# The second attention's order on TensorE: scores and value products unit by unit instead of two by two

## The chip, the cores and the metric

One Trainium2 chip, of which the kernel uses one core. The metric is the time of the core for one execution, in microseconds (us). The engines are TensorE (PE; its weight loads are listed apart, as PEld), VectorE (DVE), ScalarE (ACT), GpSimd (POOL), and SyncE (SP), which issues DMA transfers. TensorE's granted clock in the profile is 1.00 for 2.4 GHz and 0.50 for 1.2 GHz.

## The reference

Two transformer layers on x (4 batches of 256 rows of 256), each with an attention to a context of 1601 rows per batch and a mixture of experts. All is float32; a residual is added after each of the four parts.

```
x = x + L0_xattn(layernorm(x), ctx, mask)       # one head over 256 columns
x = x + L0_ffn(layernorm(x), ...)               # 16 experts, dense
x = x + L1_xattn(layernorm(x), ctx, mask, ...)  # 16 heads of 16 columns
x = x + L1_ffn(layernorm(x), ...)               # 16 experts, top 2
```

The change touches the third part alone:

```
q, k, v = proj(hs, Wq, bq), proj(at, Wk, bk), proj(at, Wv, bv)   # (B, 16, L, 16)
scores = clip(einsum('bhsd,bhtd->bhst', q, k) / 4, -50, 50)
scores = clip(where(attend, scores, -10000), -50, 50)
probs  = softmax(scores)
ctx    = einsum('bhst,bhtd->bhsd', probs, v)
delta  = layernorm(residual_scale * (ctx @ Wo.T + bo))
```

## The kernel before

The kernel is one program with one instruction list per engine; the lists are written out by hand and tied together by semaphores. Its stages are the first attention, the first experts (up to about 424 us), the second attention (424 to 647 us), and the routed experts.

The second attention works in *units*. There are 16 jobs (4 batches by 4 groups of 4 heads, `NJ`), and each job walks over the context in 13 tiles of up to 128 rows (`MT`; the last has 65), so there are 208 units (`NALL`), counted through as x or y. Per unit:

- `qk(x)` (L964): TensorE computes the scores of 4 heads as 4 matmuls (L986) of 49 rows, in the two row halves of the array: keys x 256 queries each, into a PSUM slot of two banks. There are 3 slots (`RING`), so it first waits until the exponential of unit x - 3 is done (L979).
- ScalarE (loop at L1458) takes the exponential of the 128 x 1024 scores into one of 6 buffers `p32` (L1465, `PBUF`), after the value products of unit x - 6 have left it.
- VectorE, `clip(x)` (L1980), clips it in place (L1984). The clip of the exponential stands for the clip of the scores; a column of ones in the values gives the softmax's sum.
- `pv(x)` (L1013): after the clip, TensorE multiplies it with the values: 4 matmuls in the source, 8 in the trace (L1028), each 17 columns wide, in the four column strips of the array, and accumulated over the 13 units of a job in bank 6 or 7.

TensorE runs the value products 4 units behind the scores (`PV_LAG`). Between them it does the other work of the stage, placed by unit number: `flip` (L1032) transposes a finished job's result, 7 units into the next job; `early(y)` (L940) makes queries; `between(y)` (L1080) does, for each finished batch, the transposes, the output projection (L1050), the transposes of the normalized rows (L1057), the router's logits and the ranks. ScalarE and VectorE have lists of the same names with their shares of that work, placed by unit number too, and POOL takes the reciprocal square roots of the normalization (L370 to L378). SP loads the keys of a job after the scores of three jobs before, counted on `sc_rdy`, and the values of a batch counted on `pv_done`.

Of the kernel before, what the change touches and what calls it, by code (L numbers as in the profile page):

```python
# [30 lines left out]
MT = -(-M // P)  # L31
# [24 lines left out]
NALL = NJ * MT  # L56
# [5 lines left out]
PV_LAG = 4  # L62
EVAC_AT = 3
FLIP_AT = 7
# [14 lines left out]
def build(nc, a, out, stop="D"):  # L79
# [9 lines left out]
    with ExitStack() as ctx:  # L89
# [211 lines left out]
        def at(x):  # L301

            return x // MT, x % MT

        def rows_of(m):

            return TAIL if m == MT - 1 else P
# [41 lines left out]
        def keys_in(job):  # L349

            return sum(96 + 16 * new_bar(j) for j in range(job % KSL, job + 1, KSL))
# [337 lines left out]
        def _(pe):  # L689
# [223 lines left out]
            def pair_T(q, bank):  # L913
                pe.wait_ge(ln_xn, 2 * NT + 2 * q + 2)
                for k in range(KT):
                    for j in range(2):
                        mm = pe.transpose(ps[:, bank, (2 * k + j) * P:(2 * k + j + 1) * P], xn[:, 2 * q + j, k * P:(k + 1) * P], ident[:])
                mm.then_inc(ln_T, 1)

            def first_queries(b, c, o):  # L920
                s, w = slice(b * SEQ, (b + 1) * SEQ), slice(c * P, (c + 1) * P)
                for k in range(KT):
                    mm = mm3(pe, o, wgh[:, k, w], wgl[:, k, w], xTh[:, k, s], xTl[:, k, s], k == 0, k == 1)
                mm.then_inc(Q_rdy, 1)

            def queries(n, bank):
                half, t = n // KT, n % KT
                s, w = slice(half * 512, half * 512 + 512), slice(t * P, (t + 1) * P)
                for k in range(KT):
                    mm = mm3(pe, ps[:, bank, :], wqh[:, k, w], wql[:, k, w], xTh[:, k, s], xTl[:, k, s], k == 0, k == 1)  # L930
                mm.then_inc(Q_rdy, 1)
# [8 lines left out]
            def early(y):  # L940
                if y == 0:
                    pe.wait_ge(ln_lo, 6)
                    queries(0, 7)
                elif y == 3:
                    queries(1, 6)
                elif y == 9:
                    pe.wait_ge(q_lo, 6)
                    for c in range(2):
                        first_queries(1, c, ps[:, 7, c * SEQ:(c + 1) * SEQ])
                elif y == 23:  # L950
                    pe.wait_ge(cx_rdy, 1)
                    pair_T(2, 6)
                elif y == 36:
                    pe.wait_ge(cx_rdy, 2)
                    pair_T(3, 7)
                elif y == 49:
                    pe.wait_ge(cx_rdy, 3)
                    pe.wait_ge(ln_lo, 8)
                    queries(2, 6)
                elif y == 61:  # L960
                    pe.wait_ge(cx_rdy, 4)
                    queries(3, 7)

            def qk(x):  # L964

                job, m = at(x)
                b, g = job // NG, job % NG
                if m == 0:
                    pe.wait_ge(k_in[job % KSL], keys_in(job))
                    if b == 0 and g == 0:  # L970
                        pe.wait_ge(q_lo, 4)
                    elif b == 0:
                        pe.wait_ge(q_in[g], 16 * (3 * HG + (1 if g % 2 else 0)))
                    elif b == 1 and g == 0:
                        pe.wait_ge(q_lo, 10)
                    elif b == 2 and g == 0:
                        pe.wait_ge(q_in[NG], 16 * (3 * HG * NG + 1))
                if x >= RING:
                    pe.wait_ge(p_exp, x - RING + 1)  # L979
                elif x == 1:  # L980
                    pe.wait_ge(add_rdy, 4)
                rows = rows_of(m)
                for c in range(2):
                    for t in range(2):
                        r = slice(64 * t, 64 * t + KR)
                        mm = pe.matmul(ps[0:rows, 2 * (x % RING) + t, c * SEQ:(c + 1) * SEQ], kst[r, job % KSL, c, m * P:m * P + rows],  # L986
                                       qst[r, b, 2 * g + c, :], start=True, stop=True, skip_group_check=True)
                mm.then_inc(sc_rdy, 1)

            def free_again(job):  # L990

                b, r = job // NG - 1, job % NG
                if job == 0:
                    pe.wait_ge(q_lo, 6)
                elif job == 1:
                    pe.wait_ge(q_lo, 10)
                elif job in (2, 3):
                    pe.wait_ge(ln_lo, 5 + job)
                elif job == 4:
                    pe.wait_ge(q_lo, 11)  # L1000
                if 0 < b and r == 1 and b < NB:
                    pe.wait_ge(lg_ev, min(b, NB - 2))
                if 0 <= b < NB - 1:
                    if r == 1:
                        pe.wait_ge(cT_ev, 2 * b + 2)
                    elif r == 2:
                        pe.wait_ge(dl_ev, 2 * b + 2)
                if 0 < b < NB - 1 and r == 3:
                    pe.wait_ge(pre_ev, b)
                if 0 < b and r == 0:  # L1010
                    pe.wait_ge(ln_lo, 8 + 2 * b)

            def pv(x):  # L1013

                job, m = at(x)
                b, g = job // NG, job % NG
                if m == 0:
                    if g == 0:
                        pe.wait_ge(v_in[b % 2], 16 * (b // 2 + 1))
                    if job >= 2:  # L1020
                        pe.wait_ge(cx_rdy, job - 1)
                    free_again(job)
                pe.wait_ge(p_clip, x + 1)
                rows = rows_of(m)
                for j in range(HG):
                    at_ = (m * NH + g * HG + j) * VW
                    c, t = j // 2, j % 2
                    mm = pe.matmul(ps[32 * j:32 * j + VW, 6 + job % 2, 0:SEQ], vsl[0:rows, b % 2, at_:at_ + VW],  # L1028
                                   p32[0:rows, x % PBUF, (2 * t + c) * SEQ:(2 * t + c + 1) * SEQ], start=m == 0, stop=m == MT - 1, skip_group_check=True)
                mm.then_inc(pv_done, 1)  # L1030

            def flip(job):  # L1032

                pe.wait_ge(oS_rdy, job + 1)
                for st in range(2):
                    mm = pe.transpose(ps[:, 6 + job % 2, SEQ + st * P:SEQ + (st + 1) * P], oS[:, st * P:(st + 1) * P], ident[:])
                mm.then_inc(oT_rdy, 1)
# [42 lines left out]
            def between(y):  # L1080

                b, o = y // UB - 1, y % UB
                t = 2 * b
                spare = ps[:, 6 + (y // MT - 1) % 2, :]
                if 0 < b < NB - 1 and o == 36:
                    pe.wait_ge(cx_rdy, y // MT)
                    ranks(b, t - 2, t, spare)
                if 0 < b < NB - 1 and o == 10:
                    pe.wait_ge(cx_rdy, y // MT)
                    logits(b - 1, spare)  # L1090
                if 0 <= b < NB - 1:
                    if o == 13 - 1:
                        if b:
                            pe.wait_ge(lg_ev, b)
                        else:
                            pe.wait_ge(q_lo, 12)
                        ctx_T(t, 2, spare)
                    elif o == 23:
                        pe.wait_ge(cx_rdy, y // MT)
                        ctx_out(t, 0, 2, spare[:, 0:D])  # L1100
                    elif o == 24:
                        ctx_out(t + 1, 1, 2, spare[:, D:2 * D])
                    elif o == 51:
                        pe.wait_ge(cx_rdy, y // MT)
                        rows_T(t, 2, spare)

            for x in range(0, NALL + PV_LAG, 2):
                for y in (x, x + 1):
                    if y < NALL:
                        qk(y)  # L1110
                for y in (x, x + 1):
                    early(y)
                    between(y)
                    if y >= MT + FLIP_AT and (y - FLIP_AT) % MT == 0:
                        flip((y - FLIP_AT) // MT - 1)
                    if y >= PV_LAG:
                        pv(y - PV_LAG)
            flip(NJ - 1)

            def gates(h, k, bank):  # L1120
# [1262 lines left out]
```

## Time and profile before

| | us |
|---|---|
| median of 3 runs | 746.43 |
| lowest, highest | 744.87, 751.39 |
| the profiled execution | 751.78 |
| its span in the trace | 750.0 |
| second attention, first scores to last value products | 424.3 to 647.4 |

The profile is of one execution. Times in it are microseconds from the start of its span unless ns is given. An instruction is named by its line and by the tiles that it writes and reads. An idle time in square brackets is that of the engine just before the instruction, with what ended it; "issue" means nothing that the profile shows. Where a timeline merges instructions that follow each other closely, it gives the first start, the time from there to the last end, and their count.

### The profile page before, as it was taken

To read this page: it belongs to the slowest core of one execution; us is meant where nothing else is said; L and a number is where in the kernel's file an instruction comes from. 1 tells how busy PE (TensorE), PEld (TensorE's weight loads), DVE (VectorE), ACT (ScalarE), POOL (GpSimd) and SP (SyncE) were. 2 spreads that over 40 slices of the span, in tenths; PEclk is the share of its full clock that TensorE was granted. 3 is DMA by queue.
4 is the path that set the end of the run, shared out by engine and by line. 5 is a ranking of instruction groups with operands and counts; after the bars stand their busy time and mean duration, and the time that the engine had idled before them with its cause. 6 is when DMAs were issued, how large, how long until landed. Compare 5 with 4: busy or idle time off the path is not lost.

```text
span 750.0 us, 14926 instructions
## 1 busy us (share of the span) xinstructions
PE 685.2 (91%) x5499; PEld 533.6 (71%) x5499; DVE 535.0 (71%) x1176; ACT 379.8 (51%) x564; POOL 176.5 (24%) x220
## 2 busy tenths in 40 slices
PE   4799989898889999999999699999999999989990
PEld 3799989898678888888888455455455454567870
DVE  5776747568486666666666888769788888875655
ACT  2633423244322222223232699879899999533550
POOL 5472615440000000000000050002302703542651
PEclk9999999999999999999999999979999999999995
DMA  7358474832717777677778949986888850374545
GB/s 249 123 180 264 140 263 147 272 124 90 221 47 244 225 263 244 218 214 240 256 238 147 168 82 149 207 130 99 183 157 176 126 96 2 119 296 135 158 133 189
DMA packets 55275, 131.55 MB, mean 175 GB/s; under 512 B 10007, under 2 KB 36103, under 8 KB 51631
## 3 DMA queue, kind: packets, MB, share of 16 engines
q1 hardware_dynamic: 51950, 123.32, 61.9%
q0 software_dynamic: 2256, 6.18, 2.3%
q10 hardware_dynamic: 1008, 1.25, 0.5%
q8 instruction: 38, 0.62, 0.4%
q14 instruction: 23, 0.18, 0.1%
HBM read 79.09 MB, written 48.82 MB: 171 GB/s over the span
## 4 chain that ended last, share of the span: by engine, by line
PE 73%; DVE 12%; POOL 5%; issue 4%; ACT 4%; DMA 2%; SPq 0%; POOLq 0%; DVEq 0%; ACTq 0%
PE ps L684 16%; PE ps L686 15%; PE ps L685 15%; PE ps L1028 9%; PE ps L986 6%; PE ps L1216 3%; DVE p L1984 2%; PE ps L1232 2%; PE ps L768 1%; ACT p L1465 1%; POOL nv L370 1%; POOL na L373 1%; PE ps L1200 1%; PE ps L1050 1%; POOL na L374 1%
## 5 line engine op out<-in xcount | busy, mean ns | idle before, releaser
L1465 ACT ACTIVATE p<-ps 128x1024 f32<-128x1024 f32 (+1 forms) x208 | 193.3, 1052 | 12.8 <-PE ps L986 12.8
L1984 DVE TENSOR_SCALAR p<-p 128x1024 f32<-128x1024 f32 (+1 forms) x208 | 139.0, 688 | 20.1 <-ACT p L1465 19.2
L1028 PE MATMUL ps<-p,vsl 128*17 128x256 f32 (+1 forms) x1664 | 118.0, 390 | 7.5 <-DVE p L1984 6.0
L1371 ACT ACTIVATE hh<-h 128x512 fp32r<-128x512 f32 x50 | 31.6, 632 | 132.3 <-DVE h L1851 115.3
L370 POOL TENSOR_SCALAR nv<-mv 128x2 f32<-128x2 f32 x8 | 9.5, 1187 | 354.7 <-DVE mv L1914 208.0
L986 PEld LDWEIGHTS ps<-qst,kst 49*128 49x128 f32 (+1 forms) x832 | 57.5, 184 | 49.0 <-issue 26.6
L986 PE MATMUL ps<-qst,kst 49*128 49x256 f32 (+1 forms) x832 | 81.9, 312 | 1.3 <-DVE qst L1927 0.8
L684 PE MATMUL ps<-xTh,w_hi 128*128 128x512 f32 x200 | 79.8, 399 | 1.5 <-DVE h L1847 0.9
L685 PE MATMUL ps<-xTl,w_hi 128*128 128x512 f32 x200 | 79.0, 395 | 0.0
L686 PE MATMUL ps<-xTh,w_lo 128*128 128x512 f32 x200 | 78.9, 395 | 0.0
L1028 PEld LDWEIGHTS ps<-p,vsl 128*17 128x17 f32 (+1 forms) x1664 | 35.6, 96 | 48.0 <-DVE p L1984 13.7
L1853 DVE TENSOR_TENSOR hl<-h,hh 128x512 fp32r<-128x512 f32 x50 | 34.6, 692 | 36.6 <-ACT hh L1371 36.6
L684 PE MATMUL ps<-w_hi,hh 128*128 128x256 f32 x200 | 56.6, 283 | 1.5 <-DVE hl L1853 1.5
L1847 DVE TENSOR_TENSOR h<-silu,ps 128x512 f32<-128x512 f32 x50 | 34.4, 688 | 31.9 <-PE ps L686 20.8
L685 PE MATMUL ps<-w_lo,hh 128*128 128x256 f32 x200 | 56.3, 281 | 0.0
L686 PE MATMUL ps<-w_hi,hl 128*128 128x256 f32 x200 | 56.2, 281 | 0.0
L627 POOL TENSOR_TENSOR cNl<-raw,cNh 128x1024 fp32r<-128x1024 f32 (+1 forms) x16 | 31.4, 1985 | 68.0 <-ACT cNh L1295 68.0
L684 PEld LDWEIGHTS ps<-xTh,w_hi 128*128 128x128 f32 x200 | 37.8, 189 | 9.5 <-DVE h L1847 1.7
L686 PEld LDWEIGHTS ps<-xTh,w_lo 128*128 128x128 f32 x200 | 37.6, 188 | 8.9
L685 PEld LDWEIGHTS ps<-xTl,w_hi 128*128 128x128 f32 x200 | 37.7, 189 | 6.6
L684 PEld LDWEIGHTS ps<-w_hi,hh 128*128 128x128 f32 x200 | 37.7, 188 | 4.8 <-DVE hl L1853 2.7
L1367 ACT ACTIVATE silu<-ps 128x512 f32<-128x512 f32 x50 | 30.0, 599 | 18.4 <-PE ps L686 17.8
(310 smaller groups left out, 1539.3 us busy)
## 6 DMA issues: line engine op xcount, KB each, us to landing
x_slots<-blank SPq DMA_DIRECT2D x20, 1032.0 KB, 5.9
kst<-k_hi SPq DMA_DIRECT2D x64, 200.2 KB
w_raw<-in_w SPq DMA_DIRECT2D x25, 384.0 KB, 3.6
v_one<-vst SPq DMA_DIRECT2D x4, 1768.0 KB, 10.0
vsl<-v_one SPq DMA_DIRECT2D x4, 1768.0 KB, 16.5
kst<-k_lo SPq DMA_DIRECT2D x32, 200.2 KB
raw<-in_ctxN SPq DMA_DIRECT2D x12, 512.0 KB, 5.7
e_w<-in_w SPq DMA_DIRECT2D x2, 3072.0 KB, 16.1
```

Of the source, the lines that this page charges most:

```text
L627: pool.tensor_tensor(cNl[:, c0:c0 + w, :], src, cNh[:, c0:c0 + w, :].bitcast(F32), ALU.subtract).then_inc(ctx_split, 1)
L684: e.matmul(o, lh, rh, start=first, stop=False, skip_group_check=True)
L685: e.matmul(o, lh, rl, start=False, stop=False, skip_group_check=True)
L686: return e.matmul(o, ll, rh, start=False, stop=last, skip_group_check=True)
L986: mm = pe.matmul(ps[0:rows, 2 * (x % RING) + t, c * SEQ:(c + 1) * SEQ], kst[r, job % KSL, c, m * P:m * P + rows], qst[r, b, 2 * g + c, :], ...
L1028: mm = pe.matmul(ps[32 * j:32 * j + VW, 6 + job % 2, 0:SEQ], vsl[0:rows, b % 2, at_:at_ + VW], p32[0:rows, x % PBUF, (2 * t + c) * SEQ:(2 ...
L1367: act.activation(silu[:, half, :], ps[:, 4, :], ACT.Silu).then_inc(silu_rdy, 1)
L1371: act.activation(hh[:, half, :], h32[:, half, :], ACT.Copy).then_inc(hh_rdy, 1)
L1465: act.activation(p32[0:rows, x % PBUF, :], psf[0:rows, bank * 512:bank * 512 + 1024], ACT.Exp, scale=0.25).then_inc(p_exp, 1)
L1847: dve.tensor_tensor(h32[:, half, :], silu[:, half, :], ps[:, 5, :], ALU.mult).then_inc(mul1_rdy, 1)
L1853: dve.tensor_tensor(hl[:, half, :], h32[:, half, :], hh[:, half, :].bitcast(F32), ALU.subtract).then_inc(hl_rdy, 1)
L1984: dve.tensor_scalar(t, t, CLO, CHI, ALU.max, ALU.min).then_inc(p_clip, 1)
```

## The change

TensorE's main loop over the units went in steps of two: scores of x and x + 1, then, for x and then for x + 1, the work placed at that unit (`early`, `between`, `flip`) and the value products of four units before. It now goes in steps of one: scores of y, the work placed at y, value products of y - 4. The instructions, their waits and the lists of all other engines are the same. So two units that ran as scores, scores, values, values run as scores, values, scores, values; work placed at an even unit stands between scores and values in both, and work placed at an odd unit stood between two value units and now stands between scores and values.

```diff
--- before.py
+++ after.py
@@ -1104,17 +1104,15 @@
                         pe.wait_ge(cx_rdy, y // MT)
                         rows_T(t, 2, spare)
 
-            for x in range(0, NALL + PV_LAG, 2):
-                for y in (x, x + 1):
-                    if y < NALL:
-                        qk(y)
-                for y in (x, x + 1):
-                    early(y)
-                    between(y)
-                    if y >= MT + FLIP_AT and (y - FLIP_AT) % MT == 0:
-                        flip((y - FLIP_AT) // MT - 1)
-                    if y >= PV_LAG:
-                        pv(y - PV_LAG)
+            for y in range(NALL + PV_LAG):
+                if y < NALL:
+                    qk(y)
+                early(y)
+                between(y)
+                if y >= MT + FLIP_AT and (y - FLIP_AT) % MT == 0:
+                    flip((y - FLIP_AT) // MT - 1)
+                if y >= PV_LAG:
+                    pv(y - PV_LAG)
             flip(NJ - 1)
 
             def gates(h, k, bank):
```

## Rows read from the trace of the kernel before

**Rows 1.** The page's part 1: engine, busy us, share of span, instructions.

```profile
PE 685.2 (91%) x5499; PEld 533.6 (71%) x5499; DVE 535.0 (71%) x1176; ACT 379.8 (51%) x564; POOL 176.5 (24%) x220
```

**Rows 2.** Busy time by stretch, us from the span's start; columns in its first line.

```profile
core 0: us, PE busy (x) PEld busy (x) DVE busy (x) ACT busy (x) POOL busy (x), PEclk, DMA share, GB/s
424.00:482.00 58.00, 56.03 (x680) 30.88 (x684) 48.28 (x96) 53.87 (x63) 9.59 (x28) 1.00 0.85 139
482.00:496.00 14.00, 12.63 (x92) 5.95 (x86) 7.70 (x15) 8.01 (x9) 0.00 (x0) 0.63 0.96 173
496.00:536.00 40.00, 38.59 (x506) 20.15 (x502) 33.12 (x74) 38.12 (x42) 12.19 (x28) 1.00 0.73 120
536.00:541.00 5.00, 4.01 (x32) 1.79 (x36) 4.28 (x10) 2.10 (x4) 0.00 (x0) 0.66 1.04 250
541.00:647.00 106.00, 103.40 (x1346) 55.25 (x1342) 91.21 (x212) 99.01 (x109) 32.79 (x62) 1.00 0.60 104
sum 223.00, PE 214.65 PEld 114.02 DVE 184.58 ACT 201.12 POOL 54.57; mean PE 42.93 PEld 22.80 DVE 36.92 ACT 40.22 POOL 10.91
```

**Rows 3.** The page's part 5: costliest groups, exponentials and clips.

```profile
L1465 ACT ACTIVATE p<-ps 128x1024 f32<-128x1024 f32 (+1 forms) x208 | 193.3, 1052 | 12.8 <-PE ps L986 12.8
L1984 DVE TENSOR_SCALAR p<-p 128x1024 f32<-128x1024 f32 (+1 forms) x208 | 139.0, 688 | 20.1 <-ACT p L1465 19.2
```

**Rows 4.** Timeline of ScalarE, 439.5 to 458.5: start us, us, instruction, count.

```profile
450.62 8.30 ACT L1465 ACTIVATE p<-ps 128x1024 f32<-128x1024 f32 x9
```

**Rows 5.** Timeline of TensorE's matmuls, 541.6 to 546.7.

```profile
541.77 0.74 PE L986 MATMUL ps<-qst,kst 49*128 49x256 f32 x8
542.45 1.06 PE L1028 MATMUL ps<-p,vsl 128*17 128x256 f32 x16
543.43 0.74 PE L986 MATMUL ps<-qst,kst 49*128 49x256 f32 x8
```

**Rows 6.** Timeline of TensorE's matmuls, 439.5 to 447, score groups.

```profile
442.23 0.84 PE L986 MATMUL ps<-qst,kst 49*128 49x256 f32 x8
...
444.00 0.90 PE L986 MATMUL ps<-qst,kst 49*128 49x256 f32 x8
...
445.82 0.91 PE L986 MATMUL ps<-qst,kst 49*128 49x256 f32 x8
```

**Rows 7.** Waits, 424 to 648: who for whom, us in total, times, longest.

```profile
ACT p L1465 <- PE ps L986: 12.8, 17, 1.8
...
PE ps L1028 <- DVE p L1984: 6.0, 8, 1.8
```

**Rows 8.** Timeline of TensorE's matmuls, 541.6 to 542.1 (cut inside a group).

```profile
541.77 0.51 PE L986 MATMUL ps<-qst,kst 49*128 49x256 f32 x4
```

**Rows 9.** Timeline of TensorE's matmuls, 620 to 632, a transpose between value units.

```profile
625.32 0.63 PE L1028 MATMUL ps<-p,vsl 128*17 128x256 f32 x8
625.88 0.44 PE L1036 MATMUL ps<-ident,oS 128*128 128x128 f32 x2
626.25 0.63 PE L1028 MATMUL ps<-p,vsl 128*17 128x256 f32 x8
626.80 0.74 PE L986 MATMUL ps<-qst,kst 49*128 49x256 f32 x8
```

**Rows 10.** Timeline of TensorE's weight loads, 541 to 546.

```profile
541.77 0.54 PEld L986 LDWEIGHTS ps<-qst,kst 49*128 49x128 f32 x8 [0.42 <-ACT p L1465]
...
543.43 0.54 PEld L986 LDWEIGHTS ps<-qst,kst 49*128 49x128 f32 x8 [0.42 <-issue]
```

**Rows 11.** Timeline of TensorE's matmuls, 471.9 to 474.1, a transpose before value units.

```profile
472.27 0.44 PE L1036 MATMUL ps<-ident,oS 128*128 128x128 f32 x2
...
473.62 0.74 PE L986 MATMUL ps<-qst,kst 49*128 49x256 f32 x8
```

**Rows 12.** Timeline of TensorE's matmuls: the two long waits for a clip.

```profile
485.19 0.65 PE L1028 MATMUL ps<-p,vsl 128*17 128x256 f32 x8 [1.37 <-DVE p L1984]
...
536.99 1.06 PE L1028 MATMUL ps<-p,vsl 128*17 128x256 f32 x8 [1.77 <-DVE p L1984]
```

## The prediction

> **What bounds the kernel now.** I read the page first: TensorE is busy 91% of the span and ScalarE 51% [rows 1]. These are averages over stages, so I asked for busy times of the second attention's stretch alone. Its 208 units are scored, exponentiated, clipped and multiplied with the values between 424 and 647 us. TensorE has work in 215 of those 223 us and ScalarE in 201 [rows 2]. Both look full, and the question is which of them sets the pace.
>
> ScalarE's price per unit: 208 exponentials of 1052 ns each, which overlap a little [rows 3]. Nine in a row take 8.30 us [rows 4]; (8.30 - 1.05) / 8 = 0.91 us from one to the next. 208 units need 189 us of the 221 that they are spread over.
>
> TensorE's price per unit: in the timeline, a group of two score units (8 matmuls, L986) starts at 541.77, its two value units (16, L1028) at 542.45, the next scores at 543.43 [rows 5]. That is 1.66 us for two units, 0.83 each, and it is less than ScalarE's 0.91. So in a run of plain units TensorE is ahead and waits; the reader sees this at 442 to 446, where the same groups start 1.77 and 1.82 us apart and the score group lasts 0.84 to 0.91 us in place of 0.74, because its second unit waits for a free score slot [rows 6]. But TensorE also has the transposes, projections, router logits and ranks of this stage. After each of them ScalarE has run dry (17 idle times before an exponential, 12.8 us in all [rows 7]) and TensorE catches up at 1.66. The two engines share the bound: anything that TensorE loses beyond 0.16 us per pair lands on the end.
>
> **The change, part by part.** Nothing is added or removed: the same matmuls, the same waits, the same transposes. Only TensorE's order changes, from "scores, scores, values, values" to "scores, values, scores, values". What that changes is how often TensorE passes from one kind to the other.
>
> *Step 1, the extra passages.* The matmuls themselves are cheap to count. Four score matmuls alone last 0.51 us [rows 8] and eight 0.74 [rows 5], so one more unit behind another costs 0.23. Eight value matmuls last 0.63 [rows 9] and sixteen 1.06 [rows 5]: one more unit costs 0.43. Two units of both are thus 2 x 0.66 = 1.32 of work, and the group takes 1.66. The remaining 0.34 (0.32 to 0.34 by the rounding of the rows; I take 0.33) is one round of going from scores to values and back. The same is seen on the weight loads: TensorE's loader stands idle 0.42 us before every group of score weights, named once after ScalarE and once after nothing at all [rows 10]. A reason that changes from group to group with a length that does not is a property of the passage, not a wait. The two kinds split the array differently (49 rows in two row halves; 17 columns in four column strips).
> With units alternating, two units pay two rounds: 1.66 + 0.33 = 1.99 us, 1.00 per unit. Scores run alone for units 0 to 3 and values alone for the last four in both kernels, so 102 pairs get one more round: 102 x 0.33 = 33.7 us.
>
> Here the Trainium skill has two rules that pull apart. "TensorEngine Tiling (Array Packing)", section Key Properties, says that changing the tiling mode, not merely the tile, drains the engine: by it each added passage costs, as in the sum. "TensorE: Matmul & The Clock Gate", section The mechanism, says that a weight load for row groups not in use is pulled ahead of matmuls in flight: by it the round would be nearly free and the sum near 0, a rival below. The loader's idle 0.42 is on the side of the first.
>
> *Step 2, the odd detours.* In the order before, a detour (transposes, a projection) whose unit number is even stands between scores and values, where a passage is paid anyway: 472.27 to 473.62, 1.35 us for a transpose and two value units, against 0.98 without it [rows 11, 5], 0.37 more. At an odd number it splits the two value units: 625.32 to 626.80, 1.48 us [rows 9], 0.50 more. Alternating, every detour stands between scores and values. By the code, 17 detours are at odd units where values are already under way (7 transposes of results, 4 early ones, and 6 at offsets 23 and 51 of three rounds of 52 units): 17 x 0.13 = 2.2 us back.
>
> *Step 3, what the slower TensorE covers.* At 1.00 per unit against ScalarE's 0.91, TensorE no longer waits for score slots. Such waits are worth 0.10 to 0.17 in a group [rows 6], and I find 20 groups like it at full clock in the stage's timeline and a handful of smaller ones: 4 us. If all 104 pairs had one, it would be 104 x 0.15 = 16, the upper bound; the lower is 0. It also waits less for clips: now 6.0 us in 8 waits for VectorE's clip [rows 7], most where clips queue behind router or normalization work. VectorE needs 0.69 per clip [rows 3] and gets 1.00 instead of 0.83 per unit, and four units of lag become 4.0 us instead of 3.3: I count 5 of the 6 as covered (bounds 0 and 6). ScalarE's own detours (0.6 us each) and its 12.8 us of waiting cost nothing more.
>
> *Step 4, nothing else moves.* Key and value loads are released by counts of scores and products that now come later at the same pace as their users; the two later uses of each are still in step. The normalization chain on VectorE and POOL is placed by unit number and gets more time per unit. The ring of three score slots and six probability buffers is enough: a score unit is followed within 1.05 + 0.69 + small gaps by its clip, about 2 us, and its value product comes four units, 4 us, later. The first ten units, which wait for queries, I cost at nothing either way; a wrong guess there is worth 1 us.
>
> *Step 5, the granted clock.* In two stretches it is at its lower level, 1.2 GHz (0.50): together they show as 0.63 in 482 to 496 and 0.66 in 536 to 541 [rows 2]. Each has a wait for a clip at its start (1.37 and 1.77 us [rows 12]). In 14 us there are 92 matmuls where 506 per 40 us would make 177: some 6.7 us lost, 1.4 of them the wait; in the second 32 instead of 63, 2.5 lost, 1.8 the wait. So the low clock itself costs about 6 us here. If step 3 removes the waits, this may go; if more idle array time brings more such stretches, it grows. I take no change and put both in the range.
>
> **Sum.** 33.7 - 2.2 - 4 - 5 = +22 us. The sum is made against the profiled execution: 751.8 us, its span 750.0. The median of the runs is 746.4, 0.7% below. I add the 22 to the median: **768 us**, +3.0%.
>
> **Rivals.**
> - *More cover.* The same mechanism, but nearly all the bounds of step 3 (22 us) come true: +10, or with the low clock gone too, +4 to +16. 750 to 762. Against it: from 500 us on most plain groups start 1.66 apart, with no wait left in them. Chance 0.12.
> - *The low clock spreads.* The array now stands still twice as often, if never for long. If that brings three more stretches like 482 to 496 at 5 us each, +37: 783. For it: two falls exist already. Against: both came with a wait of over 1.3 us [rows 12], while the groups stretched to 1.82 us by waiting [rows 6] lie in a stretch at 1.00 [rows 2]. Chance 0.12.
> - *The passages are hidden.* If the 0.34 is not paid per passage but once per group for another reason (the wait instructions, the first weight load after a pause), TensorE stays at 0.83, ScalarE's 0.91 holds, and the time is the same: 746. Against: the 0.42 is there before every score group. Chance 0.06.
> - *Faster.* ScalarE's 12.8 us of idling comes after detours, when TensorE has to do two score units and a detour or two value units before the next scores. Alternating, a new score unit comes after one value unit, so ScalarE is fed 0.4 us sooner after each of the 17 times and its gaps shrink: 17 x 0.43 = 7 to at most 12.8 us saved, 734 to 739. It decides only if one more round costs under about (2.2 + 9 + 7) / 102 = 0.18 us; the rows say 0.33. Chance 0.05.
>
> **Chances.** Forecast +22 (with its bounds, +13 to +31): 0.65. A measurement of this kernel can tell about 1%, 7.5 us. Slower by over 1%: 0.65 + 0.12 + most of the first rival (0.09) + 0.01 = 0.87; within 1%: 0.03 + 0.05 = 0.08; faster: 0.05. The range leaves out the hidden passages, the faster case and the lower part of the first rival (0.06), 0.17 in all: it goes from +10 (the cover of step 3 at its full 22) to +37 (the low clock's rival, which also holds the case of no cover at all, +31): 756 to 783 us.
>
> **What would show it.** In the profile after: score groups of 4 and value groups of 8 starting about 1.00 us apart per unit; exponentials spaced 1.00 us with ScalarE idle 0.1 before nearly each, put down to L986; over 190 weight loader idles of about 0.42 before L986; VectorE waits of L1028 near 1 us in all; the stage 243 to 247 us in place of 223; everything before 424 and after the stage unchanged. Step 1 is wrong if units come 0.83 to 0.91 apart. Step 3 is wrong in size if the stage grows by over 30 at full clock, step 5 if the granted clock shows longer stretches at 1.2 GHz or none.

## The result: 22 us slower, as forecast

| | us | granted clock |
|---|---|---|
| before, median of 4 runs | 747.8 (744.9 to 751.4) | |
| after, median of 4 runs | 769.9 (768.6 to 773.5) | 0.967 to 0.974 |
| the profiled execution of after | 770.4, span 768.5 | 0.971 |

The ratio is 1.030 with a 95% interval of 1.024 to 1.036. 768 was forecast, in a range of 756 to 783.

The page of after, part 1, against [rows 1]; and of part 5 the exponentials, against the first of [rows 3]:

```profile
PE 709.2 (92%) x5499; PEld 532.3 (69%) x5499; DVE 536.6 (70%) x1176; ACT 390.8 (51%) x564; POOL 173.4 (23%) x220
```

```profile
L1463 ACT ACTIVATE p<-ps 128x1024 f32<-128x1024 f32 (+1 forms) x208 | 203.9, 1027 | 19.8 <-PE ps L986 19.6
```

TensorE has 24 us more of busy time, and ScalarE's idle time before exponentials grew from 12.8 to 19.8 us: it now waits for scores more, though it has the same 208 exponentials. (The line numbers of the other engines' lists are two lower than before.) The timeline of TensorE's matmuls after, to be read beside [rows 5]; columns are start, length, instruction and count:

```profile
562.55 0.50 PE L986 MATMUL ps<-qst,kst 49*128 49x256 f32 x4
562.98 0.63 PE L1028 MATMUL ps<-p,vsl 128*17 128x256 f32 x8
563.54 0.50 PE L986 MATMUL ps<-qst,kst 49*128 49x256 f32 x4
563.97 0.63 PE L1028 MATMUL ps<-p,vsl 128*17 128x256 f32 x8
564.53 0.51 PE L986 MATMUL ps<-qst,kst 49*128 49x256 f32 x4
```

Scores of one unit, values of one, scores of the next. From 562.55 to 563.54 and to 564.53 it is 0.99 us a unit; two units took 1.66 before. The work in such a unit is 0.23 + 0.43. From the start of the scores to the values it is 0.43, 0.20 more than the work, and from the values to the scores 0.56, 0.13 more: the two halves of a round of passages. The same holds for the whole stage: in the 167 steps from one unit's scores to the next with nothing but scores and values in them, none takes more than 0.99 us, so TensorE waits in none of them. The weight loads of the same stretch, against [rows 10]:

```profile
563.54 0.30 PEld L986 LDWEIGHTS ps<-qst,kst 49*128 49x128 f32 x4 [0.42 <-issue]
...
564.52 0.30 PEld L986 LDWEIGHTS ps<-qst,kst 49*128 49x128 f32 x4 [0.42 <-ACT p L1463]
```

And the waits of the stage (in total, times, longest), against [rows 7]:

```profile
PEld ps L986 <- ACT p L1463: 56.2, 132, 0.7
...
PEld ps L986 <- issue: 32.4, 74, 1.2
ACT p L1463 <- PE ps L986: 19.6, 30, 2.7
...
PE ps L1028 <- DVE p L1982: 0.5, 1, 0.5
```

The first two rows are the loader's idle times before score weights: 206 times and 88.6 us. In the same view of before they are 106 times and 46.7 us. The hundred that came are 0.42 us each, like the old ones. The wait of TensorE's matmuls for a clip fell from 6.0 us in 8 times to 0.5 in one.

The granted clock by stretch (us, busy times of PE, PEld, DVE, ACT and POOL, clock, DMA share, GB/s), against [rows 2]:

```profile
424.00:437.00 13.00, 10.79 (x47) 7.94 (x46) 7.70 (x14) 7.54 (x12) 0.00 (x0) 0.64 0.84 123
437.00:665.00 228.00, 227.05 (x2612) 104.23 (x2616) 181.43 (x394) 206.35 (x217) 53.90 (x119) 1.00 0.65 116
```

There is no stretch at 1.2 GHz in the middle of the stage any more, and one at its start, while TensorE makes the queries. The stage, from the first start of a score matmul to the last start of a value matmul, is 427.9 to 665.2, 237.3 us; before it was 424.3 to 647.0, 222.7. So this pair of profiles differs by 14.6 us in the stage, 3.6 ahead of it, where nothing was changed, and nothing behind it. Why the medians are 22 apart and the stages 15 is taken up with e11 and e12.

### The profile page after: what moved, and what is told of

The parts are those of the page before. It is cut to its first block, busy times and chain, and to the rows that moved or that the text cites. A ratio compares the mean times of both kernels' runs of the same rounds, so it can differ in the third digit from the quotient of the medians.

```text
span 768.5 us, 14926 instructions
## 1 busy us (share of the span) xinstructions
PE 709.2 (92%) x5499; PEld 532.3 (69%) x5499; DVE 536.6 (70%) x1176; ACT 390.8 (51%) x564; POOL 173.4 (23%) x220
## 4 chain that ended last, share of the span: by engine, by line
PE 82%; DVE 8%; ACT 3%; DMA 3%; issue 2%; SPq 1%; POOL 0%; DVEq 0%; POOLq 0%; ACTq 0%
PE ps L684 15%; PE ps L1028 15%; PE ps L685 15%; PE ps L686 15%; PE ps L986 12%; PE ps L1214 3%; PE ps L1230 2%; PE ps L1050 1%; PE ps L768 1%; PE ps L1198 1%; DMA raw<-in_ctxT 1%; PE ps L1036 1%; ACT hh L1369 1%; DMA comb_b<-comb_rows 1%; DVE h L1845 1%
## 5 line engine op out<-in xcount | busy, mean ns | idle before, releaser
L1463 ACT ACTIVATE p<-ps 128x1024 f32<-128x1024 f32 (+1 forms) x208 | 203.9, 1027 | 19.8 <-PE ps L986 19.6
L1028 PE MATMUL ps<-p,vsl 128*17 128x256 f32 (+1 forms) x1664 | 129.7, 385 | 1.4 <-issue 0.9
L986 PEld LDWEIGHTS ps<-qst,kst 49*128 49x128 f32 (+1 forms) x832 | 61.0, 183 | 88.6 <-ACT p L1463 56.2
L986 PE MATMUL ps<-qst,kst 49*128 49x256 f32 (+1 forms) x832 | 104.2, 330 | 1.0 <-DVE qst L1925 1.0
L370 POOL TENSOR_SCALAR nv<-mv 128x2 f32<-128x2 f32 x8 | 6.2, 770 | 370.3 <-DVE mv L1912 212.6
L1028 PEld LDWEIGHTS ps<-p,vsl 128*17 128x17 f32 (+1 forms) x1664 | 27.9, 95 | 32.6 <-issue 8.0
```

The source lines that it names most:

```text
L1463: act.activation(p32[0:rows, x % PBUF, :], psf[0:rows, bank * 512:bank * 512 + 1024], ACT.Exp, scale=0.25).then_inc(p_exp, 1)
```

## The experiments

Theory A is the prediction's: each round of passages between scores and values costs TensorE about 0.33 us, and TensorE sets the pace. B: waits make the loss. C: the price is paid only once after a wait. D, for larger groups: the three score slots run dry. A time is given with its ratio to before, measured beside it, and the 95% interval of that; e5, e7 and e8 have none.

**e1: each unit cut in halves, by heads.**

```diff
             for y in range(NALL + PV_LAG):
                 if y < NALL:
-                    qk(y)
+                    qk(y, (0,))
+                if y >= PV_LAG:
+                    pv(y - PV_LAG, (0, 1))
+                if y < NALL:
+                    qk(y, (1,))
...
                 if y >= PV_LAG:
-                    pv(y - PV_LAG)
+                    pv(y - PV_LAG, (2, 3))
```

> The order after the change, and each unit cut once more: half of its scores, half of the value products of four units before, the other half of each. Matmuls, weights and waits for other engines stay. Two rounds of passages per unit in place of one, about 206 more. Theory A (every round between scores and values costs TensorE about 0.33 us, and TensorE sets the pace): 206 x 0.33 = 68 us more than after the change, 770 + 68 = 838, at least 825. Rival B (the loss comes from waits: unit by unit, each engine waits for the one before it, and the passages themselves are free or hidden): the waits are the same as after the change, so 770 within 6. Rival C (the passage costs only at the first weight load after a wait): also near 770, at most 780.

Measured: 930.0 us, ratio 1.237 (1.229 to 1.245). That is 160 us above after, where A said 68 and B and C nothing. TensorE's timeline:

```profile
602.42 0.38 PE L986 MATMUL ps<-qst,kst 49*128 49x256 f32 x2
602.74 0.61 PE L1029 MATMUL ps<-p,vsl 128*17 128x256 f32 x4
603.28 0.38 PE L986 MATMUL ps<-qst,kst 49*128 49x256 f32 x2
```

A half takes 0.86 (602.42 to 603.28), a unit 1.72. Four value matmuls now take as long as eight: the four heads use four column strips side by side, and two heads leave two strips empty. So 0.43 per unit is the edit's own, 208 x 0.43 = 89 us, and the 71 that are left are near A's 68, though part of them is the clock's (0.956 in this profile, 0.971 in after). By the rows one more round is 1.72 - 0.99 - 0.43 = 0.30 us. The design mixed two costs, so it was done again.

**e2: every second pair alternates.** The edit against before, cut:

```diff
             for x in range(0, NALL + PV_LAG, 2):
+                groups = ((x, x + 1),) if x % 4 else ((x,), (x + 1,))
+                for ys in groups:
...
```

> The order before, with every second pair of units alternating: 51 more rounds of passages instead of 102. Theory A: 51 x 0.33 = 17 us more for TensorE, less about 1 for detours and less the waits that it covers; the cover is used up by the first rounds (about 7 to 9 us of waits for score slots and clips in the profile before), so +7 to +11 over before: 755 to 759. A strictly proportional loss would be half of 22, 759. Rival B (waits of the alternating order): the pair groups between them let the engines catch up, so 748 to 752.

Measured: 756.5 us, 1.0085 (1.0037 to 1.0134): +6 to its own reference of 750.3. The time is in A's range; the size of the step is a little below its +7 to +11 and above B's. Half of the rounds cost clearly less than half of the 22, as it must be if the first ones are covered by waits.

**e3 and e4: groups of three and of four.** The loop steps by 3 (from 0) or by 4 (from -2, so that the first group has two). Shown is e3, cut.

```diff
-            for x in range(0, NALL + PV_LAG, 2):
-                for y in (x, x + 1):
+            for x in range(0, NALL + PV_LAG, G):
+                ys = range(x, min(x + G, NALL + PV_LAG))
+                for y in ys:
...
```

> Groups of three units: three scores, three value products. 70 rounds in place of 104 before. Theory A: TensorE needs 34 x 0.33 = 11 us less than before and is below ScalarE's 0.91 us per unit (0.66 + 0.11 = 0.77); the time falls only by what TensorE held up in catching up after detours, 3 to 8 us: 740 to 745. Rival D (the three score slots hold 2.7 us of ScalarE's work, and a block of three values with a detour behind it is longer, so ScalarE runs dry more often than it gains): 748 to 755.

> Groups of four units (the first group has two, so that the detours fall where the other engines expect them). 53 rounds. Theory A: TensorE needs 51 x 0.33 = 17 us less than before, but the fourth score unit waits for the exponential three before it, and the next scores come only after four value units, 1.7 + 0.33 us, or with a detour up to 3.7 us, against 2.7 us of work in the slots: ScalarE loses up to 1 us at each longer detour, about 12 of them. 740 to 750. Rival D: ScalarE runs dry at every detour, the transposes too: 755 to 765.

Measured: e3 752.2 us, 1.002 (0.997 to 1.007); e4 780.8 us, 1.040 (1.034 to 1.047). A's gain came for neither. e3 is in D's range (748 to 755); e4 is above both ranges, 16 us above the upper end of D's. TensorE's score groups in e3, and its two waits with ScalarE over the stage:

```profile
607.65 0.80 PE L986 MATMUL ps<-qst,kst 49*128 49x256 f32 x8
608.88 0.50 PE L986 MATMUL ps<-qst,kst 49*128 49x256 f32 x4 [0.42 <-ACT p L1467]
```

```profile
ACT p L1467 <- PE ps L986: 9.5, 18, 1.8
...
PE ps L986 <- ACT p L1467: 8.0, 23, 1.0
```

The scores of the third unit (608.88) come 1.23 us after those of the first: a slot has to come free. TensorE stands idle for slots 8.0 us in 23 times, which it hardly did before, and ScalarE's waiting fell only from 12.8 to 9.5. So the 11 us that rounds gave back became waits; ScalarE's 0.91 a unit is now the bound in plain stretches. In e4 there is another one, in ScalarE's timeline and in the waits over the whole execution:

```profile
604.00 3.77 ACT L1467 ACTIVATE p<-ps 128x1024 f32<-128x1024 f32 x4 [0.32 <-PE ps L1028]
608.47 2.96 ACT L1467 ACTIVATE p<-ps 128x1024 f32<-128x1024 f32 x3 [0.69 <-PE ps L1028]
```

```profile
PE ps L986 <- ACT p L1467: 32.8, 81, 0.8
...
ACT p L1467 <- PE ps L1028: 22.7, 49, 2.9
```

Four exponentials take 3.77 us and then ScalarE stands 0.32 to 0.69 us until a value product (L1028) frees one of the six probability buffers: 49 times, 22.7 us. D named the slots; it is both slots and buffers, and the buffers are what neither expectation had. Of groups of 1 to 4 none is faster than two; three is the same within its interval.

**e5 and e6: the cut made again, by queries, with a control.** e6 cuts each unit's value products into two halves of 128 queries that follow each other; e5 puts half of the scores between them. Shown are two lines of e5, cut at their ends; the loop over the units is cut up as in e1. In e6 `hs` is `range(2)` and the loop over the units is that of after.

```diff
-                for j in range(HG):
+                for h, j in [(h, j) for h in hs for j in range(HG)]:
...
-                    mm = pe.matmul(ps[32 * j:32 * j + VW, 6 + job % 2, 0:SEQ], ...
+                    mm = pe.matmul(ps[32 * j:32 * j + VW, 6 + job % 2, n0:n1], ...
```

> As e1, but the value products are cut by queries (128 and 128 for all four heads) instead of by heads. In e1 each half used two of the four column strips, so the value products themselves took twice as long, which the expectation had left out. Here all four strips stay in use. About 206 more rounds of passages than after the change. Theory A: 206 x 0.33 = 68 us more than e6, the control with the same cut value products and no extra rounds: about 838 to 845 if the control is at 770 to 775. Rival B and C: within 6 us of the control.

> The order after the change, with each unit's value products cut into two halves of 128 queries that follow each other directly: twice as many matmuls of half the width, no extra round. All theories: the array's time is the same, so 770 to 775; if a matmul has a fixed price of its own that shows here, up to 785. It is the base for e5.

Measured: e6 812.6 us, 1.088 (1.077 to 1.099), where 770 to 785 was expected. e5 906.8 us; its four runs lie between 871 and 920 with granted clocks of 0.926 to 0.856, so its time can't be compared and only rows at one clock can. e6 at 2.4 GHz, then at 1.2 GHz:

```profile
600.37 0.51 PE L986 MATMUL ps<-qst,kst 49*128 49x256 f32 x4
600.80 0.63 PE L1029 MATMUL ps<-p,vsl 128*17 128x128 f32 x16
601.37 0.51 PE L986 MATMUL ps<-qst,kst 49*128 49x256 f32 x4
```

```profile
441.52 0.79 PE L986 MATMUL ps<-qst,kst 49*128 49x256 f32 x4
...
443.23 0.79 PE L986 MATMUL ps<-qst,kst 49*128 49x256 f32 x4
```

At full clock a unit takes 1.00 us, as in after: cutting costs the array nothing. At 1.2 GHz it takes 1.71. What the control lost, 43 us, is for the most part the clock: over its four runs it is 0.918 to 0.945, where after has 0.966 to 0.980. The rest is idle time of TensorE: in e6 it stands 13.6 us in 9 times before its matmuls for nothing that the profile shows, up to 3.3 us at a time, where after has 0.9 us. e5 at 2.4 GHz (the first fence) and at 1.2 GHz:

```profile
541.52 0.38 PE L986 MATMUL ps<-qst,kst 49*128 49x256 f32 x2
541.84 0.41 PE L1030 MATMUL ps<-p,vsl 128*17 128x128 f32 x8
542.18 0.39 PE L986 MATMUL ps<-qst,kst 49*128 49x256 f32 x2
```

```profile
600.54 0.58 PE L986 MATMUL ps<-qst,kst 49*128 49x256 f32 x2
...
601.61 0.58 PE L986 MATMUL ps<-qst,kst 49*128 49x256 f32 x2
```

At full clock half a unit takes 0.66 (541.52 to 542.18), a unit 1.32; e6, with the same matmuls and one round fewer, takes 1.00. The round costs 0.32. That is theory A's price, on rows, without the strips' mistake; B and C are out, as nothing waits between these groups. The times point the same way, roughly: e5's fastest run is 871.2 us at a clock of 0.926, and e6's runs at 0.935 and 0.918 (813 and 823) make about 818 there, some 53 apart where A said 68 and B and C at most 6.

**e7 and e8: is it the data type?** Scores as float32 in both orders; the operands, cut:

```diff
-                        mm = pe.matmul(..., kst[r, job % KSL, c, m * P:m * P + rows],
-                                       qst[r, b, 2 * g + c, :], ...)
+                        mm = pe.matmul(..., kst[r, job % KSL, c, m * P:m * P + rows].bitcast(F32),
+                                       qst[r, b, 2 * g + c, :].bitcast(F32), ...)
```

> The order after the change, with the score matmuls read as float32 in place of float32r, which the value products are already: both kinds have one data type and still split the array differently. The scores take more passes, about 0.86 us per unit of work in place of 0.23, so only the difference to e8 is read. If the passage belongs to the change of the array's split: each round still costs about 0.33, TensorE is the only bound, nothing covers it, and e7 is 102 x 0.33 - 2 = 31 us above e8 (27 to 36). If it belongs to the change of data type: e7 is 0 to 10 above e8.

> The order before, with float32 scores. 208 units with 0.63 us more work each, 131 us, of which little is covered: 750 + 131 less 5 to 15 of waits, 862 to 880. It is the base for e7, and as there is no wait for ScalarE left in either, e7 less e8 is the price of step 1 and 2 without the cover of step 3.

One run each: e7 893.6 us, e8 864.9 us. e7 is 28.8 us above e8 (27 to 36 expected of the array's split, 0 to 10 of the data type). Matmuls of e7, one weight load of it, and matmuls of e8:

```profile
604.79 1.13 PE L986 MATMUL ps<-qst,kst 49*128 49x256 f32 x8
605.86 0.62 PE L1028 MATMUL ps<-p,vsl 128*17 128x256 f32 x8
606.41 1.13 PE L986 MATMUL ps<-qst,kst 49*128 49x256 f32 x8
```

```profile
604.79 0.73 PEld L986 LDWEIGHTS ps<-qst,kst 49*128 49x128 f32 x8 [0.42 <-issue]
```

```profile
604.47 2.00 PE L986 MATMUL ps<-qst,kst 49*128 49x256 f32 x16
606.39 1.06 PE L1028 MATMUL ps<-p,vsl 128*17 128x256 f32 x16
607.38 2.00 PE L986 MATMUL ps<-qst,kst 49*128 49x256 f32 x16
```

Two units alternating take 3.24 (twice 1.62, 604.79 to 606.41), in a pair 2.91: 0.33 for a round, the same as with mixed types, and the loader's 0.42 is still there. So the data type isn't what is paid for. The stages are 423.4 to 788.3 (364.9 us) and 426.7 to 760.1 (333.4): 31.5 apart, with next to nothing to cover it: the two matmul waits of e8's stage are 1.3 us together.

That the split of the array is the cause is what is left of the two. With the rule of the Trainium skill ("TensorEngine Tiling (Array Packing)", section Key Properties) that a change of tiling mode drains the engine, the loader's idle 0.42 us agrees. Another reading would be that a weight load waits whenever running matmuls use its rows. Against it is a row of the loader in before, beside [rows 5]:

```profile
542.44 0.56 PEld L1028 LDWEIGHTS ps<-p,vsl 128*17 128x17 f32 x16
```

The value weights of a pair's second unit are loaded within these 0.56 us, while the first unit's value products run, though both use all the rows. No run here had equal splits with everything else kept, so that the split is the cause remains argued; that the round costs 0.33 us and is no wait is shown.

**e9 and e10: versions that might beat both.** e9 puts both detours of a pair between scores and values; e10 does so too, with groups of three where there is no long detour and of two where there is.

```diff
                 for y in (x, x + 1):
                     early(y)
                     between(y)
                     if y >= MT + FLIP_AT and (y - FLIP_AT) % MT == 0:
                         flip((y - FLIP_AT) // MT - 1)
+                for y in (x, x + 1):
                     if y >= PV_LAG:
                         pv(y - PV_LAG)
```

> The order before, but with the detours of both units of a pair between the scores and the value products, so none stands between two value units. By step 2 of the prediction 17 detours cost 0.13 less each, 2.2 us of TensorE's time. Theory A: 1 to 2 us below before, 0.998 in ratio, at the edge of what can be told. Rival: detours that wait for VectorE or ScalarE now hold up two value units in place of one: the same or up to 3 us slower.

> Groups of three units where there is no long detour, of two where there is one, and all detours between scores and values. About 75 rounds in place of 104, 29 x 0.33 = 10 us less for TensorE, plus 2 for the detours. By e3 (groups of three everywhere: the same time as before, so that what the rounds gave went into waits for score slots and idle ScalarE) I expect part of the gain to stay where the long detours no longer follow a block of three: theory A 740 to 746 where before is 750, ratio 0.987 to 0.995. Rival D (the slack of the three slots decides everywhere): 0.997 to 1.005.

Measured: e9 748.6 us, 1.0061 (1.0026 to 1.0096); e10 750.7 us, 1.0081 (1.0046 to 1.0117); before 746.5 in 23 runs. Neither beats it. e9, matmuls around a projection, and a wait that the kernel before doesn't have:

```profile
606.54 0.74 PE L986 MATMUL ps<-qst,kst 49*128 49x256 f32 x8
607.21 1.13 PE L1050 MATMUL ps<-wo_raw,wq_raw 128*128 128x256 f32 x4
608.27 1.06 PE L1028 MATMUL ps<-p,vsl 128*17 128x256 f32 x16
609.26 0.73 PE L986 MATMUL ps<-qst,kst 49*128 49x256 f32 x8
```

```profile
PE ps L1057 <- DVE xe L2046: 3.6, 3, 2.2
```

The pair takes 2.72 (606.54 to 609.26), where before one with the same projection between its value units takes 2.83 (614.05 to 616.88 in the timeline of before): step 2's 0.13 is seen as 0.11. But TensorE now waits 3.6 us in 3 times for normalized rows before their transposes (L1057), with two value units behind it. That is the rival of the expectation, and its range. e10 is slower than both of its ranges. Its waits are

```profile
ACT p L1476 <- PE ps L986: 10.1, 12, 1.6
PE ps L986 <- ACT p L1476: 7.2, 23, 0.5
```

so of what it saves in rounds, 7.2 us go into waits for score slots, as in e3. Both are a little slower than before. Their clocks are a little lower (medians 0.973 and 0.974 against 0.977), and with the low clock taken out as below (time times granted clock) e9 is 727.9 us, e10 732.4 and before 728.8. So e9's loss is no more than the clock's; where e10's 3.6 come from isn't settled.

**e11 and e12: both kernels again.** (In the expectation, 224.3 is a slip for 424.3.)

> The kernel before, unchanged, with a second profile. The first profile has two stretches at 1.2 GHz in the stage, and its stage (224.3 to 647.0 starts, 222.7 us) is 14.6 us shorter than after, while the medians are 22 apart. If such stretches come by chance (the clock theory), this profile has another set of them and the stage is 214 to 223 us, shorter the less low clock it has; a stage free of them is 214 to 217 us, about 22 below after. If they belong to this order's long clip waits, they stand again near 485 and 537.

> The kernel after, unchanged, with a second profile. Ratio to before 1.026 to 1.034. Theory A: the stage is 233 to 238 us, units 1.00 us apart, clip waits about 1 us, whatever the clock did; low clock at most at the start of the stage, where TensorE waits for the queries. If the unit by unit order itself brings the clock down, at least one stretch of it stands in the middle of the stage, and it is over 240.

Measured: e11 748.7 us, 1.0004 (0.9967 to 1.0041); e12 769.6 us, 1.0285 (1.0239 to 1.0331). The stretches of e11, and then of e12:

```profile
418.00:432.00 14.00, 12.22 (x68) 9.01 (x68) 9.37 (x16) 9.45 (x13) 0.00 (x0) 0.63 0.96 133
432.00:645.00 213.00, 205.77 (x2619) 109.49 (x2612) 179.48 (x397) 194.91 (x217) 57.30 (x120) 1.00 0.70 124
```

```profile
418.00:434.00 16.00, 12.57 (x92) 6.56 (x92) 10.16 (x22) 10.09 (x12) 2.22 (x8) 0.80 0.53 90
434.00:661.00 227.00, 225.93 (x2573) 104.66 (x2569) 178.87 (x385) 202.52 (x213) 49.49 (x113) 0.99 0.65 116
```

| profile | first score | last value | stage | low clock in it |
|---|---|---|---|---|
| before | 424.3 | 647.0 | 222.7 | near 485 and 537 |
| e11, the same | 421.9 | 642.0 | 220.1 | at the start |
| after | 427.9 | 665.2 | 237.3 | at the start |
| e12, the same | 418.2 | 658.7 | 240.5 | at the start |

The waits for clips at L1028 stand in e11 as before (5.8 us in 9 times, the longest 1.8), but the low clock of 485 and 537 doesn't: these waits alone don't bring it. e11's 220.1 is in the range of 214 to 223, above the 214 to 217 of a stage with no low clock in its middle. e12 has none in the middle of the stage, but missed the expected 233 to 238 by 2.5 us. The stages differ by 14.6 in the first pair, by 20.4 in the second. The part ahead of the stage, untouched, starts it anywhere from 418 to 428. Most of this scatter is the clock's: the stage times its own mean granted clock (0.969, 0.984, 0.986, 0.979) is 215.9, 216.6, 233.9 and 235.3 us, 17 to 19 apart in every pairing of a before with an after. One pair of profiles as it stands can't give a difference of 22 to better than some 5 us; the medians can.

## Why the prediction was right

**Step 1, the price of a round: right.** 0.33 was taken from three rows. It came out as 0.32 in after (2 x 0.99 - 1.66), 0.32 in e5 against e6, 0.33 in e7 against e8. The number of rounds is right too: the loader has 100 idle times of 0.42 more, 102 were forecast. The stages of e7 and e8, where nothing covers, differ by 31.5; steps 1 and 2 gave 33.7 - 2.2 = 31.5.

**Step 2, the odd detours: the price right, but alone it brought nothing.** 0.11 for 0.13 on rows of e9. In e9 it was eaten up by a detour that comes earlier and waits.

**Step 3, the cover: too small.** This is the term of the sum that was mis-sized: 9 us were forecast (4 of slots, 5 of clips), and 12.5 to 14.5 of the 31.5 were covered.

The one bound comes from two profiles in which the clock is full from the first value product to the last: e11 takes 210.8 us for that (431.2 to 642.0) and after 227.8 (437.4 to 665.2), 17.0 apart. e8 and e7 are 31.5 apart in the same stretch (324.5 and 356.0), so 14.5 were covered. The other bound comes from all runs, with the low clock taken out: a run's time times its granted clock is what it would be if each microsecond at 1.2 GHz counted for a half. That is 728.9 us for before (mean of 60 runs) and 747.9 for after (10 runs), 19.0 apart, so 12.5 were covered. This is an estimate; at 1.2 GHz a unit of e6 takes 1.71 times as long and not twice, so it takes out a little too much.

Where the cover lay can be read pair by pair. e8 has the same order as e11 and hardly a wait, and its plain pairs are 1.26 us longer (2.92 and 1.66). Against e8's pairs less 1.26, e11's are 14.1 us longer in sum: 8.6 in the 12 pairs in which TensorE stands idle before value products, nearly always for a clip, 1.0 in the first pair, and 4.5 in all others, which are the waits for slots. So the slots were right (4), and the clips were not (5, with 6 as the bound). The forecast took their price from the idle time that the profile shows, 6.0 us. A pair of before shows why that is too little:

```profile
581.70 0.74 PE L986 MATMUL ps<-qst,kst 49*128 49x256 f32 x8
582.37 0.63 PE L1028 MATMUL ps<-p,vsl 65*17 65x256 f32 x8
583.69 0.63 PE L1028 MATMUL ps<-p,vsl 128*17 128x256 f32 x8 [0.70 <-DVE p L1984]
584.25 0.74 PE L986 MATMUL ps<-qst,kst 49*128 49x256 f32 x8
```

It takes 2.55 us (581.70 to 584.25) in place of 1.66, 0.89 more, and the idle time shown is 0.70.

**Step 4:** the part behind the last value product is the same, 103 us in both. From the first score to the first value product it is 7.0 us in before and 8.3 in e12, both with little low clock there, and 9.3 in e11 and 9.5 in after, both with much. In e8 and e7, whose stages have no low clock, it is 9.0 and 8.9: no cost of the order shows at the start.

**Step 5, the clock: right as to chance, wrong as to zero.** By the same reckoning the two kernels lose 18.1 and 21.4 us to the low clock: about 3 of the 22 are the clock's. So 22 = 19 + 3, where 22 + 0 was forecast. The two errors, each about 3 us, cancel: that the order costs some 20 us was understood, and that the forecast hit 22 was luck. The cover in e2 shows the same shape: half of the rounds cost 6 us, the other half 16.

**The signs.** Units 0.99 us apart, 206 idle times of the loader and 0.5 us of waits for clips are as forecast. Two signs failed. The stage was to take 243 to 247 us; it took 237.3 and 240.5, as the cover was larger and part of the 22 lies outside, in the clock. And ScalarE was to stand idle 0.1 us before nearly every exponential. It does so 30 times in all, 19.6 us; between, its timeline in after shows eight exponentials in a row in 7.95 us (from 563.10), 0.99 apart with no idle time, as each lasts 1.03.

**The rivals.** Hidden passages and a faster kernel are excluded by the rows of after. The prediction tied the first of them to weight loads for rows not in use too; the value products use all 128 rows, so in the step from values to scores that case doesn't arise. More cover was right in direction and about a third of its way. The low clock spreading was not seen in after, but it was in e6 and e5, so it was no idle fear.

## What to carry to other kernels

Before splitting or interleaving two kinds of matmul, measure from the timeline what a change between them costs: length of a group less the lengths that one more unit adds inside it. Here it is 0.33 us a round, half of a unit's work, and grouping by two paid it half as often. Of the groups tried here, two was enough: it makes TensorE (0.83 a unit) just faster than ScalarE (0.91), and beyond it the gain turned into waits for slots (e3) and buffers (e4). Price a wait by how much longer the group around it takes from start to start, not by the idle time shown. And when an edit cuts matmuls, check that it leaves as many strips of the array busy as before (e1).

## What was not expected of the hardware

Cutting the value matmuls from 256 to 128 columns left a unit's time at full clock as it was (1.00 us, e6) and yet cost 43 us, for the most part as the granted clock fell to 0.918 to 0.945 from 0.966 to 0.980. In the profile of e6 it falls four times after the first value products, at 438.6, 523.9, 561.4 and 640.0 us, each time within 2 us of the end of a wait of TensorE (2.43, 3.28, 1.65 and 1.28 us) that the profile puts down to nothing. The waits before value matmuls, in total, times, longest:

```profile
PE ps L1029 <- issue: 8.6, 5, 3.3
```

What they wait for is open. In before, the falls at 485.7 and 536.9 stand at the end of waits of 1.37 and 1.77 us [rows 12]. But such a wait doesn't always bring one: e11 has one of 1.8 us and no fall. And a fall doesn't need one: in e5 the clock fell at 591 and stayed at 0.50 to 809, 2 us before the last value product. TensorE was busy in all of the 50 us from 550 to 600, and no wait stands in its timeline there. The clock is not a matter of waits alone.

At 1.2 GHz a unit of e6 takes 1.71 us in place of 1.00, and half a unit of e5 1.07 in place of 0.66: less than twice as long, so part of such a group doesn't scale with the clock.
